# The order of the middle groups' steps on four engines, in a four-layer kernel on one Trainium2 core

## The chip, the core and the metric

The kernel runs as one program on one core of a Trainium2 chip. The metric is the device time of one execution in microseconds (us). The engines are named as the profile names them: PE (TensorE; PEld its weight loads), DVE (VectorE), ACT (ScalarE), POOL (GpSimd), SP (the queue that loads and stores). Each works through its own instructions in order and waits for the others at semaphores.

## What is computed

Four layers over an input of 16 sequences of 256 tokens with 128 features. Each layer's output is normed and added to its input. Cut to what matters:

```python
x = x + norm(conv(norm(x)))          # a long convolution along the tokens, one decaying complex mode per feature
x = x + norm(moe(norm(x)))           # 8 routed experts (the best 2 by softmax) and a shared one, silu(x Wg) * (x Wu) Wd
x = x + norm(attention(norm(x)))     # 16 heads of 64, q and k of unit length, ALiBi, causal, 2 null keys
x = x + norm(four_experts(norm(x)))  # router (best 2 of 4) over a gated MLP, two chains of matrices, a gelu MLP
```

In the fourth layer all four experts are computed for every token and weighed by `pick1`, which is zero for those not chosen.

## The kernel before

The 16 sequences are worked in 8 groups of 2 (512 tokens, four tiles of 128). A group passes through the four layers, whose steps bear the letters `e` (convolution), `l` (routed experts), `a` (attention) and `f` (four experts). The layers of different groups are interleaved: while the list plays group g's attention, it plays the fourth layer of group g-1 and the expert layer and convolution of groups g+1 and g+2. For each engine a list of step names, written out by hand in tables at the top of the file, sets the order of its instructions. `play` (L702) goes through a list and calls each step; `plan` (L707) plays `PROLOGUE` and `FIRST` once, `MIDDLE` five times (groups 1 to 5), then `LAST_L`, `LAST_A` and `LAST_F`:

```python
for i in range(1, G - 2):
    play(steps, table(MIDDLE[name]), e=i + 2, l=i + 1, a=i, f=i - 1)
```

A step does the same in whatever place it stands, and waits for its inputs at semaphores; the lists set only what is queued ahead of what. The steps that matter here:

- `a_m`, `a_k`, `a_v` (PE, three products of 512 columns for each half): projections to queries, keys and values, into three PSUM banks in turn; `a_t` turns the unit queries. ACT empties each bank.
- `l_turn3`: PE turns the normed tile of the expert layer (L1784), ACT copies it (L1112), DVE takes the rest below fp32r (L1477). The routing and all of the expert layer follow from it. It needs `l_norm` (DVE, L1399 `xn<-x`).
- `l_route`, `l_pick`, `l_coef`: router products on PE (L1778, L1779), the best two on DVE (L1495 to L1505), their weights (L1511 to L1525).
- `f_out.t` (t = 0 to 3): PE computes the outputs of the four experts for tile t (L2229 to L2235), DVE adds them up weighted (L1723, four instructions). The first of these starts from the biases that POOL's `f_bias` has weighed and added (L983, L987). `f_bias` needs the routing weights (`f_pick`, DVE, L1693 to L1705) and `l_norm`.
- `f_end_stats`, `f_end`: norm of the fourth layer's sum and the residual (L1399 `x4m`, L1404).
- `a_nexp` (DVE, L1592 and L1594, then ACT, L1183): the null keys' exponentials; `a_nT` turns them.
- `a_scores.c` (c = 0 to 7, a unit of four heads of one sequence): PE's scores in four 64x64 tiles (L2036, L2042), ACT's exponentials (L1199 to L1208), POOL's causal masks and the addition of the late keys (L952, L962). `a_mix.c`: PE's sums and mixes (L2091 to L2105), then DVE's division (L1609 to L1623). PE's scores of the next unit need ACT's exponentials of this one; PE's mix of the next unit needs DVE's division of this one.
- `l_g`, `l_u`, `l_c` (PE) with `l_hg`, `l_hu`, `l_hc` (DVE): gate, up and coefficient of the expert layer, five times; `l_c` is one product over 72 rows (L1930). `l_down`, `a_out`: the output products.
- `e_stats`, `e_apply`, `e_scan`, `e_sum`: norm and scan of the convolution two groups ahead; POOL's `e_scan` is two products (L923). `a_keep` is POOL's copy of a layer's input (L933). `a_kss`, `a_ss` are POOL's roots for keys and queries (L943, L937).

At the end of the list the attention input is normed (`l_aapply`), turned (`l_x`, L1951), split (`l_xl`, DVE, L1477 `xaT_lo`), and the next `a_m.0` starts.

Of the kernel before, what the change touches and what calls it, by code (L numbers as in the profile page):

```python
# [83 lines left out]

MIDDLE = {
    "PE": """
a_m.0 a_m.1 a_k.0 f_turn.0 f_turn.1 a_null f_ce.0 f_ce.1 a_k.1 f_sw.0 f_me.0 a_kr.0 a_t.0 f_ceT a_m.2 f_sw.1 a_k.2
f_relu.0 a_k.3 f_sw.2 a_t.1 a_m.3 f_relu.1 a_kr.1 f_sw.3 a_kt f_ce2 f_me.1 l_turn2 a_v.0 a_t.2 f_ml.0 a_v.1 f_ml.1
a_t.3 f_ce2T f_ml.2 f_ml.3 a_v.2 a_v.3 l_turn3 f_out.0 l_route f_out.1 a_scores.0 a_nT f_out.2 l_g.0 f_out.3
a_scores.1 l_u.0 l_g.1 l_cT a_mix.0 a_scores.2 a_mix.1 e_turn1 l_u.1 a_scores.3 l_g.2 l_c.0 l_u.2 a_mix.2 a_scores.4  # L90
a_mix.3 l_g.3 l_u.3 a_scores.5 l_c.1 l_g.4 a_mix.4 a_scores.6 l_u.4 l_c.2 a_mix.5 l_c.3 a_scores.7 a_mix.6 l_down.0
l_down.1 l_down.2 a_mix.7 l_down.3 a_out.0 a_out.1 l_x.0 l_x.1
""",
    "DVE": """
f_stats.0 f_stats.1 f_apply.0 f_apply.1 a_ss.0 f_turn.0 a_null f_turn.1 f_ce f_route a_u.0 f_ce_apply f_hid.0 a_ss.1
a_ss.2 f_hid.1 a_u.1 f_pick a_u.2 f_hid.2 a_ss.3 a_kss f_hid.3 f_ce2 l_turn2 a_u.3 f_ce2_apply l_res l_norm l_turn3
e_stats a_nexp l_route l_pick l_coef f_out.0 a_nT f_out.1 l_hg.0 f_out.2 f_out.3 f_end_stats e_apply a_mix.0 l_hu.0
l_hg.1 a_mix.1 l_cT l_hu.1 e_scan a_mix.2 l_hg.2 l_hu.2 a_mix.3 l_hc.0 l_hg.3 l_hc.1 e_sum l_hu.3 a_mix.4 l_hc.2
a_mix.5 l_hg.4 l_hu.4 l_hc.3 a_mix.6 f_end l_dstats.0 a_mix.7 l_end.0 l_dstats.1 l_astats.0 l_end.1 a_o.0 l_astats.1
a_end.0 l_aapply.0 l_aapply.1 a_o.1 l_xl.0 l_xl.1 a_end.1  # L100
""",
    "ACT": """
a_m.0 a_m.1 f_turn.0 f_turn.1 a_k.0 a_k.1 f_me.0 f_sw.0 a_t.0 f_pick f_ceT a_m.2 f_sw.1 a_k.2 f_relu.0 a_k.3 a_t.1
f_sw.2 a_m.3 a_ks f_relu.1 f_sw.3 a_v.0 a_t.2 f_ml.0 a_v.1 f_ml.1 a_t.3 f_ce2T f_ml.2 f_ml.3 a_v.2 f_me.1 l_turn3
a_nexp a_v.3 l_exp a_scores.0 l_g.0 a_scores.1 l_g.1 l_cT a_scores.2 a_scores.3 l_g.2 a_scores.4 l_g.3 a_scores.5
a_scores.6 l_g.4 a_scores.7 l_x.0 l_x.1
""",
    "POOL": """
f_stats.0 f_stats.1 a_ss.0 f_ce a_ss.1 a_ss.2 f_ce_apply a_ss.3 f_ce2 l_turn2 a_kss.0.0 l_res a_kss.0.1 f_bias
a_kss.1.0 e_stats a_kss.1.1 a_scores.0 a_keep a_scores.1 a_scores.2 a_scores.3 e_scan a_scores.4 f_end_stats  # L110
a_scores.5 a_scores.6 a_scores.7 l_dstats.0 l_dstats.1 l_astats.0 a_o.0 l_astats.1 a_o.1
""",
}

# [2162 lines left out]
```

## Time and profile before

| what | us |
|---|---|
| median of 3 runs (lowest to highest) | 929.02 (928.15 to 929.4) |
| the profiled execution | 928.41 |
| its span, first to last instruction | 926.6 |
| what lies around the span | 1.8 |
| busy: PE / DVE / POOL / ACT | 860.1 / 779.7 / 587.7 / 586.2 |
| mean granted TensorE clock | 0.991 of full speed |

The span holds a prologue, the first group, the five middle groups of some 106.5 us each, and the three closing lists. Busy time is what an engine's instructions cover; matmuls are pipelined, so a busy PE need not be at its peak. DMA plays a part at the start only: over the span HBM is used at 11 GB/s.

### The profile page before, as it was taken

What the parts mean: (1) busy time and instruction counts of PE and PEld (TensorE: products, weight loads), DVE (VectorE), ACT (ScalarE), POOL (GpSimd) and SP (SyncE); (2) the same over time, 40 slices, a digit from 0 to 9 for tenths busy, and PEclk for the clock granted to TensorE, in tenths of its full rate; (3) what the DMA queues carried; (4) which work ended last, traced back from release to release, by engine and by line L of the source; (5) the groups of instructions that cost most, each with busy time, mean ns of one, the idle gap of its engine ahead of it and who ended that gap; (6) DMA issues with size and microseconds to landing.
All of it is one profiled execution on the core that took longest, in us unless ns stands there. A gap on an engine that the chain in (4) does not pass through costs nothing.

```text
span 926.6 us, 25509 instructions
## 1 busy us (share of the span) xinstructions
PE 860.1 (93%) x10110; PEld 700.6 (76%) x10110; DVE 779.7 (84%) x2457; ACT 586.2 (63%) x1255; POOL 587.7 (63%) x632
## 2 busy tenths in 40 slices
...
DMA packets 22008, 11.73 MB, mean 13 GB/s; under 512 B 7552, under 2 KB 21248, under 8 KB 21760
## 3 DMA queue, kind: packets, MB, share of 16 engines
...
## 4 chain that ended last, share of the span: by engine, by line
PE 49%; DVE 38%; ACT 7%; issue 4%; POOL 2%; DMA 0%; DVEq 0%; ACTq 0%; POOLq 0%
PE bank L1771 8%; PE bank L1772 7%; PE bank L1773 7%; PE bank L1784 5%; DVE x4m L1723 3%; PE bank L2036 3%; DVE qT L1623 2%; DVE mixed L1620 2%; PE bank L2042 2%; PE bank L1999 2%; PE bank L2204 1%; DVE bank L1609 1%; DVE xn L1399 1%; PE bank L2211 1%; DVE conv L1451 1%
## 5 line engine op out<-in xcount | busy, mean ns | idle before, releaser
L937 POOL TENSOR_TENSOR rnorm<-sumsq,minus_half 128x16 f32<-128x16 f32 x32 | 95.4, 2990 | 55.6 <-DVE sumsq L1574 55.3
L943 POOL TENSOR_TENSOR rnorm<-unit,minus_half 128x16 f32<-128x16 f32 x32 | 93.1, 2916 | 3.1 <-DVE unit L1580 3.1
L1202 ACT ACTIVATE square<-bank,bias_k,rnorm 128x256 f32<-128x256 f32 x128 | 65.7, 570 | 44.8 <-PE bank L2036 44.8
L2042 PE MATMUL bank<-qT,kT 64*64 64x64 f32 (+1 forms) x1024 | 82.9, 253 | 5.6 <-ACT unit L1208 3.3
L2036 PE MATMUL bank<-qT,kT 64*64 64x256 f32 (+1 forms) x1024 | 84.4, 358 | 0.0
L952 POOL TENSOR_SCALAR_AFFINE_SELECT square<-square 128x256 f32<-128x256 f32 x128 | 61.8, 509 | 34.3 <-ACT square L1208 34.3
L1132 ACT ACTIVATE xaT_hi<-bank 128x256 fp32r<-128x256 f32 x16 | 6.0, 384 | 115.3 <-PE bank L1951 114.7
L952 POOL TENSOR_SCALAR_AFFINE_SELECT unit<-unit 128x256 f32<-128x256 f32 x128 | 48.5, 407 | 37.9 <-ACT unit L1208 37.9
L2042 PEld LDWEIGHTS bank<-qT,kT 64*64 64x64 f32 x1024 | 51.9, 132 | 20.8 <-ACT unit L1208 6.9
L2118 PE MATMUL bank<-w_out,qT 128*128 128x128 f32 x512 | 62.8, 276 | 1.5 <-DVE qT L1623 1.5
L1202 ACT ACTIVATE unit<-bank,bias_k,rnorm 128x256 f32<-128x256 f32 x96 | 51.5, 575 | 17.7 <-PE bank L2036 16.3
L2118 PEld LDWEIGHTS bank<-w_out,qT 128*128 128x128 f32 x512 | 59.7, 192 | 2.3 <-DVE qT L1623 1.7
L2036 PEld LDWEIGHTS bank<-qT,kT 64*64 64x64 f32 x1024 | 55.1, 132 | 5.3
L1208 ACT ACTIVATE unit<-bank,bias_k,rnorm 128x128 f32<-128x128 f32 x128 | 52.8, 479 | 0.0
L1208 ACT ACTIVATE square<-bank,bias_k,rnorm 128x128 f32<-128x128 f32 x128 | 52.4, 473 | 0.0
L1175 ACT ACTIVATE val<-bank 128x512 f32<-128x512 f32 x64 | 37.1, 595 | 24.2 <-PE bank L1773 22.0
L1784 PEld LDWEIGHTS bank<-ident,unit 128*128 128x128 f32 x296 | 34.6, 143 | 18.0 <-DVE unit L1588 11.7
L901 POOL TENSOR_TENSOR n_d_rstd<-n_d_var,minus_half 128x2 f32<-128x2 f32 x16 | 11.7, 732 | 57.3 <-DVE n_d_var L1415 57.2
L1571 DVE TENSOR_REDUCE sumsq<-square 128x16 f32<-128x1024 f32 x32 | 38.9, 1215 | 10.1 <-ACT square L1148 10.1
L1141 ACT ACTIVATE unit<-bank 128x512 f32<-128x512 f32 x64 | 36.9, 605 | 16.5 <-PE bank L1773 15.3
L1784 PE MATMUL bank<-ident,unit 128*128 128x128 f32 x296 | 40.6, 279 | 6.2 <-DVE unit L1588 5.3
L1623 DVE TENSOR_TENSOR qT<-bank,mixed 128x512 f32<-128x512 f32 x64 | 44.2, 691 | 2.2
...
## 6 DMA issues: line engine op xcount, KB each, us to landing
...
```

Of the source, the lines that this page charges most:

```text
L937: pool.tensor_tensor(rnorm[:, 1, t, :], sumsq[:, t % 2, :], minus_half[:], ALU.pow).then_inc(a_root.sem, 1)
L943: pool.tensor_tensor(rnorm[:, 0, ts, hs], k_sumsq[:, ts, hs], minus_half[:, hs].unsqueeze(1).to_broadcast([P, 2, H // 2]), ALU.pow).then_i ...
L952: pool.affine_select(out=pd, in_=pd, compare_op=ALU.is_ge, fill=0.0, base=0, pattern=[[0, 2], [step, P]], channel_multiplier=-step).then_i ...
L1202: last = act.activation(early(pr, j), k0, ACT.Exp, bias=bias_k0[:, h:h + 1], scale=by)
L1208: last = act.activation(late(pr, j), bank[2][:, 2 * P * s + P * j:2 * P * s + P * (j + 1)], ACT.Exp, bias=bias_k1[:, h:h + 1], scale=by)
L1771: mm(dst, left.hi, right.hi, start=True, stop=False)
L1772: mm(dst, left.hi, right.lo, start=False, stop=False)
L1773: return mm(dst, left.lo, right.hi, start=False, stop=True)
L1784: last = nc.tensor.transpose(dst[:, t * P:(t + 1) * P], src(t), ident[:])
L2036: return mm(bank[s][cs, 2 * P * (i + 1) - n:2 * P * (i + 1)], kT[rs, p, 2 * P * b + 64 * k:2 * P * b + 64 * k + 64], qT[rs, p, 2 * P * (b ...
L2042: return mm(bank[2][cs, 2 * P * s + P * i:2 * P * s + P * i + n], kT[rs, p, tile1 + 64 * k:tile1 + 64 * k + 64], qT[rs, p, tile1:tile1 + n ...
L2118: mm(out_bank(g, h)[:, ts], outT[:, c, ts], w_out[:, c, :], start=(c == 0), stop=False)
```

## The change

The table `MIDDLE` is replaced by another order of the same steps, for PE, DVE, ACT and POOL. Nothing else changes: the other lists, the steps, the scores in four tiles and the coefficients over 72 rows stay. The order in which the banks for `a_m`, `a_k`, `a_t` and `a_v` are taken in turn (it is read from PE's list) comes out the same, and so does the mix ahead of which PE turns the next convolution's input (`e_turn1`, after two mixes). The lines of the diff that the text speaks of:

```diff
 MIDDLE = {
     "PE": """
-a_m.0 a_m.1 a_k.0 f_turn.0 f_turn.1 a_null f_ce.0 f_ce.1 a_k.1 f_sw.0 f_me.0 a_kr.0 a_t.0 f_ceT a_m.2 f_sw.1 a_k.2
+a_m.0 a_m.1 a_null a_k.0 f_turn.0 f_turn.1 f_ce.0 f_ce.1 a_k.1 f_sw.0 f_me.0 a_kr.0 a_t.0 a_m.2 f_ceT f_sw.1 a_k.2
...
-a_t.3 f_ce2T f_ml.2 f_ml.3 a_v.2 a_v.3 l_turn3 f_out.0 l_route f_out.1 a_scores.0 a_nT f_out.2 l_g.0 f_out.3
+f_ce2T a_t.3 a_v.2 f_ml.2 f_ml.3 a_v.3 f_out.0 l_turn3 f_out.1 l_route a_scores.0 l_g.0 f_out.2 f_out.3 a_nT
...
     "DVE": """
...
-e_stats a_nexp l_route l_pick l_coef f_out.0 a_nT f_out.1 l_hg.0 f_out.2 f_out.3 f_end_stats e_apply a_mix.0 l_hu.0
+l_turn3 e_stats f_out.0 l_route l_pick f_out.1 l_hg.0 l_coef f_out.2 f_out.3 f_end_stats a_nT a_mix.0 l_hg.1 e_apply
...
     "POOL": """
-f_stats.0 f_stats.1 a_ss.0 f_ce a_ss.1 a_ss.2 f_ce_apply a_ss.3 f_ce2 l_turn2 a_kss.0.0 l_res a_kss.0.1 f_bias
-a_kss.1.0 e_stats a_kss.1.1 a_scores.0 a_keep a_scores.1 a_scores.2 a_scores.3 e_scan a_scores.4 f_end_stats
+f_stats.0 f_stats.1 a_ss.0 f_ce a_ss.1 a_ss.2 f_ce_apply a_ss.3 a_kss.0.0 f_ce2 l_turn2 a_kss.0.1 l_res f_bias
+a_kss.1.0 e_stats a_kss.1.1 a_scores.0 a_scores.1 a_scores.2 a_scores.3 e_scan a_keep a_scores.4 a_scores.5
```


On PE, ahead of the score units, where the third middle group leaves the value projections and turns the expert layer's input (`xn`). Before:

```order
L1771 MATMUL bank<-w_kv_hi,xaT_hi 128x512
L1772 MATMUL bank<-w_kv_lo,xaT_hi 128x512
L1773 MATMUL bank<-w_kv_hi,xaT_lo 128x512
L1784 MATMUL bank<-ident,xn 128x128 x4
L2229 MATMUL bank<-w_sw,mixed 128x128 x4
L2231 MATMUL bank<-w_c,mixed 128x128 x2
L2233 MATMUL bank<-w_gen,x4m 128x128
L2235 MATMUL bank<-w_ml,square 128x128 x4
```


And now:

```order
L1771 MATMUL bank<-w_kv_hi,xaT_hi 128x512
L1772 MATMUL bank<-w_kv_lo,xaT_hi 128x512
L1773 MATMUL bank<-w_kv_hi,xaT_lo 128x512
L2229 MATMUL bank<-w_sw,mixed 128x128 x4
L2231 MATMUL bank<-w_c,mixed 128x128 x2
L2233 MATMUL bank<-w_gen,x4m 128x128
L2235 MATMUL bank<-w_ml,square 128x128 x4
L1784 MATMUL bank<-ident,xn 128x128 x4
```


The four products of `f_out.0` (L2229 to L2235) have gone ahead of the turning of `xn`.

On DVE, from `l_norm` (L1399 `xn<-x`) of the same group to the first weighted sums (L1723). Before:

```order
L1399 TENSOR_SCALAR xn<-x,n_l_mv,n_l_rstd 128x128 x4
L1477 TENSOR_TENSOR xlT_lo<-bank,xlT_hi 128x512
L1389 BN_STATS n_x_six<-xin 128x6 x4
L1392 BN_AGGR n_x_mv<-n_x_six 128x2 x4
L1394 TENSOR_SCALAR n_x_var<-n_x_mv 128x4
L1592 TENSOR_TENSOR null_s<-null_s,rnorm 128x128
L1594 SCALAR_TENSOR_TENSOR null_s<-null_s,bias_null 128x128
L1495 TENSOR_REDUCE logit<-bank 128x32
L1501 MAX top<-logit 128x8 x4
L1504 MAX_INDEX idx<-top,logit 128x8 x4
L1505 TENSOR_TENSOR exp<-top 128x32
L1511 CAST idf<-idx 128x8
```


And now:

```order
L1399 TENSOR_SCALAR xn<-x,n_l_mv,n_l_rstd 128x128 x4
L1592 TENSOR_TENSOR null_s<-null_s,rnorm 128x128
L1594 SCALAR_TENSOR_TENSOR null_s<-null_s,bias_null 128x128
L1477 TENSOR_TENSOR xlT_lo<-bank,xlT_hi 128x512
L1389 BN_STATS n_x_six<-xin 128x6 x4
L1392 BN_AGGR n_x_mv<-n_x_six 128x2 x4
L1394 TENSOR_SCALAR n_x_var<-n_x_mv 128x4
L1723 SCALAR_TENSOR_TENSOR x4m<-bank,pick,ce_rows 128x128
L1723 SCALAR_TENSOR_TENSOR x4m<-bank,pick,x4m 128x128 x3
L1495 TENSOR_REDUCE logit<-bank 128x32
L1501 MAX top<-logit 128x8 x4
L1504 MAX_INDEX idx<-top,logit 128x8 x4
```


`a_nexp` (L1592, L1594) has gone ahead of `l_turn3` (L1477), and `f_out.0` (L1723) ahead of the router's reduction and pick (L1495 to L1505).

On POOL, from the query roots to the biases (L983, L987) of the same group. Before:

```order
L937 TENSOR_TENSOR rnorm<-sumsq,minus_half 128x16
L894 TENSOR_TENSOR n_c_rstd<-n_c_var,minus_half 128x4
L894 TENSOR_TENSOR n_y_rstd<-n_y_var,minus_half 128x4
L943 TENSOR_TENSOR rnorm<-unit,minus_half 128x2x8
L894 TENSOR_TENSOR n_l_rstd<-n_l_var,minus_half 128x4
L943 TENSOR_TENSOR rnorm<-unit,minus_half 128x2x8
```


And now:

```order
L937 TENSOR_TENSOR rnorm<-sumsq,minus_half 128x16
L943 TENSOR_TENSOR rnorm<-unit,minus_half 128x2x8
L894 TENSOR_TENSOR n_c_rstd<-n_c_var,minus_half 128x4
L894 TENSOR_TENSOR n_y_rstd<-n_y_var,minus_half 128x4
L943 TENSOR_TENSOR rnorm<-unit,minus_half 128x2x8
L894 TENSOR_TENSOR n_l_rstd<-n_l_var,minus_half 128x4
```


The first key root (L943) has gone ahead of the roots for `f_ce2` (`n_c_rstd`) and `l_turn2` (`n_y_rstd`), and the second ahead of that for `l_res` (`n_l_rstd`).

## Rows read from the trace of the kernel before

**Rows 1.** The page's head: busy time of each engine (share of the span).
```profile
PE 860.1 (93%) x10110; PEld 700.6 (76%) x10110; DVE 779.7 (84%) x2457; ACT 586.2 (63%) x1255; POOL 587.7 (63%) x632
```

**Rows 2.** Three middle groups: start:end, length, busy us of PE, PEld, DVE, ACT, POOL, clock.
```profile
140.70:247.10 106.40, 103.45 (x1296) 84.22 (x1295) 95.23 (x300) 72.30 (x156) 74.22 (x76) 1.00 0.02 5
247.11:353.25 106.14, 103.09 (x1246) 84.17 (x1245) 95.42 (x303) 70.24 (x150) 71.79 (x73) 1.00 0.02 7
...
459.65:566.76 107.11, 104.35 (x1249) 85.69 (x1248) 95.87 (x303) 70.26 (x150) 71.91 (x73) 0.98 0.02 7
```

**Rows 3.** The same view, the two parts of the third middle group.
```profile
369.47:410.65 41.18, 41.03 (x217) 30.79 (x218) 35.88 (x121) 35.38 (x67) 26.04 (x15) 1.00 0.03 8
410.65:475.80 65.15, 62.36 (x1032) 53.67 (x1031) 59.72 (x181) 34.85 (x83) 45.97 (x59) 1.00 0.02 6
```

**Rows 4.** PE's longest wait in four middle groups: us in total, times, longest.
```profile
PE bank L1771 <- DVE xaT_lo L1477: 3.1, 4, 0.8
```

**Rows 5.** Order of time, third middle group, DVE: start, us, instruction [idle before it].
```profile
409.42 1.12 DVE L1399 TENSOR_SCALAR xn<-x,n_l_mv,n_l_rstd 128x128 f32<-128x128 f32 x4 [1.12 <-POOL n_l_rstd L894]
411.91 0.69 DVE L1477 TENSOR_TENSOR xlT_lo<-bank,xlT_hi 128x512 fp32r<-128x512 f32 x1 [1.38 <-ACT xlT_hi L1112]
...
414.21 0.28 DVE L1592 TENSOR_TENSOR null_s<-null_s,rnorm 128x128 f32<-128x128 f32 x1
...
415.69 0.21 DVE L1495 TENSOR_REDUCE logit<-bank 128x32 f32<-128x64 f32 x1
...
416.90 1.23 DVE L1505 TENSOR_TENSOR exp<-top 128x32 f32<-128x32 f32 x1
...
419.12 0.29 DVE L1522 TENSOR_TENSOR pick<-pick,prob 128x32 f32<-128x32 f32 x2
...
452.89 0.69 DVE L1539 TENSOR_TENSOR unit<-unit,bank 128x512 f32<-128x512 f32 x1 [0.44 <-PE bank L1930]
...
459.57 2.50 DVE L1399 TENSOR_SCALAR x4m<-x4m,n_f_mv,n_f_rstd 128x128 f32<-128x128 f32 x4
```

**Rows 6.** The same view, PE: start of `f_out.0`, and of the router's products.
```profile
411.08 1.06 PE L2229 MATMUL bank<-w_sw,mixed 128*128 128x128 f32 x8
...
413.46 0.26 PE L1778 MATMUL bank<-w_router,xlT_hi 128*128 128x16 f32 x1
```

**Rows 7.** The same view, POOL: roots, biases (first and last of five), the copy.
```profile
396.77 2.91 POOL L937 TENSOR_TENSOR rnorm<-sumsq,minus_half 128x16 f32<-128x16 f32 x1 [2.28 <-DVE sumsq L1574]
401.27 1.01 POOL L894 TENSOR_TENSOR n_c_rstd<-n_c_var,minus_half 128x4 f32<-128x4 f32 x1 [1.59 <-DVE n_c_var L1394]
...
412.21 1.05 POOL L983 TENSOR_TENSOR ce_rows<-row_out,pick 128x512 f32<-128x512 f32 x1
...
416.82 1.27 POOL L987 TENSOR_TENSOR ce_rows<-ce_rows,x 128x512 f32<-128x512 f32 x1
418.05 2.91 POOL L943 TENSOR_TENSOR rnorm<-unit,minus_half 128x16 f32<-128x16 f32 x1
...
427.56 0.61 POOL L933 COPY x<-x2n 128x512 f32<-128x512 f32 x1
```

**Rows 8.** The same view, DVE, in the group behind the middle ones (list LAST_L).
```profile
731.58 1.11 DVE L1399 TENSOR_SCALAR xn<-x,n_l_mv,n_l_rstd 128x128 f32<-128x128 f32 x4 [0.60 <-POOL n_l_rstd L894]
...
738.89 0.35 DVE L1723 SCALAR_TENSOR_TENSOR x4m<-bank,pick,ce_rows 128x128 f32<-128x128 f32 x1 [2.68 <-POOL ce_rows L987]
...
772.38 0.47 DVE L1609 STREAM_TRANSPOSE bank<-bank 128x256 f32<-128x256 f32 x1 [1.80 <-PE bank L2094]
...
776.39 1.44 DVE L1399 TENSOR_SCALAR x4m<-x4m,n_f_mv,n_f_rstd 128x128 f32<-128x128 f32 x4
```

**Rows 9.** The same view, DVE, first middle group: the pick's last step, its successor.
```profile
204.07 0.17 DVE L1505 TENSOR_TENSOR exp<-top 128x32 f32<-128x32 f32 x1
204.28 1.12 DVE L1511 CAST idf<-idx 128x8 f32<-128x8 uint32 x1
```

**Rows 10.** As rows 2: where the fourth group begins its projections.
```profile
475.80:480.00 4.20, 4.20 (x12) 3.29 (x13) 3.59 (x16) 2.54 (x5) 1.70 (x3) 0.60 0.00 0
```

More of the change, by code:

```diff
@@ L92 @@
-l_down.1 l_down.2 a_mix.7 l_down.3 a_out.0 a_out.1 l_x.0 l_x.1
+a_m.0 a_m.1 a_null a_k.0 f_turn.0 f_turn.1 f_ce.0 f_ce.1 a_k.1 f_sw.0 f_me.0 a_kr.0 a_t.0 a_m.2 f_ceT f_sw.1 a_k.2
+a_k.3 f_relu.0 f_sw.2 a_t.1 a_m.3 a_kr.1 f_relu.1 f_sw.3 a_kt f_ce2 a_v.0 l_turn2 f_ml.0 f_ml.1 a_t.2 a_v.1 f_me.1
+f_ce2T a_t.3 a_v.2 f_ml.2 f_ml.3 a_v.3 f_out.0 l_turn3 f_out.1 l_route a_scores.0 l_g.0 f_out.2 f_out.3 a_nT
+a_scores.1 l_u.0 l_g.1 a_mix.0 a_scores.2 a_mix.1 l_u.1 e_turn1 l_g.2 a_scores.3 a_mix.2 l_u.2 l_cT a_scores.4
```

27 lines of the change are left out of this document (12 added, 15 removed).

## The prediction

> **What bounds the kernel now.** I read the page first, then the stretches group by group, then the waits, then the order in time of one group. By the page PE is busy 860 of 926.6 us and DVE 780 [rows 1], so neither is free as an average. The five middle groups, whose lists change, each take 106.1 to 107.1 us, with PE busy about 103.4 and DVE about 95.5 [rows 2]. They repeat, so I work in one of them, from its first query projection (369.47) to that of the next (475.80).
>
> It has two parts [rows 3]. From 369.47 to 410.65 PE is busy 41.03 of 41.18 us and DVE 35.88: PE alone sets the pace, until it turns the normed tile in `l_turn3`. From there to 475.80 DVE is busy 59.72 of 65.15 us as the profile counts, and its order of time has two marked gaps, 0.31 and the 0.44 of [rows 5]; the chain of waits follows DVE there. PE is nearly as full (62.36). Its longest wait there is 0.8, at the handover to the next group, once in each of four [rows 4]. So a step moved out of the second part helps if it is DVE's, and a step moved into the first part hurts if it is PE's. This change does one of each.
>
> **The change part by part.** No instruction is added or removed; 5 groups are reordered. All terms are us per group.
>
> 1. *PE computes `f_out.0` ahead of `l_turn3`.* Before, `l_turn3` starts at 410.65 [rows 3], `f_out.0` runs from 411.08 and the router's products start at 413.46 [rows 6]. These 2.4 us now lie at the end of the part that PE sets, and all that DVE does after `l_turn3` starts as much later: **+2.4**.
>
> 2. *The other swaps ahead of `l_turn3`* (`a_null`, `f_ceT`, `f_relu`, `f_me.1`, `f_ml`, `a_v` change places). PE's sum is the same; PE has 0.15 us to gain there (41.18 less 41.03). It can lose: POOL now takes the root `a_kss.0.0` ahead of `f_ce2`'s. Such a root takes 2.91, and POOL had 1.59 idle ahead of `f_ce2`'s at 401.27 [rows 7], so that this one comes 1.3 later. DVE has `a_u.3` to do in between, and PE's `f_ce2T`, which needs what follows, has a dozen products queued ahead of it. Bounds -0.15 to +1.3, taken **0**.
>
> 3. *DVE does `a_nexp` ahead of `l_turn3`.* From 414.21 to 415.69 it took 1.48 [rows 5]; now it runs while PE is still busy with term 1, where DVE waits anyway. **-1.5**.
>
> 4. *`f_out.0` goes ahead of the router's pick on DVE.* The last step of `l_pick` took 1.23 us [rows 5] and 0.17 in the first middle group [rows 9]; it began at 416.90, beside POOL's addition of the biases that began at 416.82 and took 1.27 [rows 7]. Since `f_out.0` needs the sum of these biases, `l_pick` now comes after that addition, beside the root that POOL takes next (2.91). Beside such a root DVE is not held: `l_coef`'s two products of 419.12, with two SBUF inputs each, took 0.29 together [rows 5] within the root of 418.05 to 420.96 [rows 7]. **-1.1**, bounds -1.1 to 0. The Trainium skill (SBUF — State Buffer, "Who interferes with whom") says that a DVE instruction with two SBUF inputs and a POOL instruction that reads SBUF exclude each other for the whole instruction. That agrees with the 1.23 beside the addition; for the root it says the opposite of the row above, and speaks against this change. By it the term would be about +0.9, as `l_coef` would have to wait (last rival).
>
> 5. *`f_out.0` waits for POOL's biases.* They take 412.21 to 418.05, 5.84 us [rows 7], and need `l_norm`, which ended at 410.54 (409.42 + 1.12) [rows 5]. In the group behind the middle ones, whose list has the same order here, `f_out.0` began at 738.89, 6.2 us after `l_norm`'s end (731.58 + 1.11), having waited 2.68 [rows 8]. Now `l_norm` ends between 410.54 and 411.5, an estimate: `f_pick` is put ahead of it, where DVE waited 1.12, and some of term 2's 1.3 arrives. So the sum is ready at 416.7 to 417.7. DVE gets there at 411.91 + 2.4 + 2.3 (`l_turn3` and `e_stats`, 411.91 to 414.21) = 416.6. Bounds +0.1 to +1.1, taken **+0.5**.
>
> 6. *`f_end` ahead of `a_mix.6`.* It took 2.50 us [rows 5], and 1.44 where the last-but-one list has it at the same place [rows 8]. POOL's masks of the last unit now fall beside it, so I take half: **-0.5**, bounds -1.1 to 0.
>
> 7. *The chain scores, exponentials, masks, mix.* POOL's copy `a_keep` (0.61) [rows 7] moves from ahead of unit 1 to between the products of `e_scan` and unit 4's masks, and PE's `a_mix.4` is queued behind it, and DVE's behind that. PE's `a_mix.0` also finds `a_nT` directly ahead of it on DVE, where six steps had stood between. Bounds: -0.75, if nothing new waits and the 0.31 and 0.44 go, to +1.8, the longest wait of this chain in the next list [rows 8]. Taken **+0.6**, the copy.
>
> ACT's and SP's moves are covered: ACT is busy 70 of 106 us [rows 2], and no DMA is nearer its use than before. The end of the group (`l_dstats.1` ahead of `l_end.0`, `l_aapply.0` ahead of `a_end.0`) has the same DVE steps before the next projections: 0.
>
> Sum: 2.4 + 0 - 1.5 - 1.1 + 0.5 - 0.5 + 0.6 = **+0.4 a group, +2.0 for five**. The profiled execution took 928.41, 0.61 under the median of the runs shown (929.02), and so would take 930.4; against the median that is **931.0 us**.
>
> **Rivals.**
>
> *Faster: DVE's relief all arrives.* `f_out.0` finds the biases ready (+0.1), `f_end` runs in 1.44 (-1.1), and the chain gains nothing and loses nothing: 2.4 - 1.5 - 1.1 + 0.1 - 1.1 = -1.2 a group, **923.0**. PE's own work allows it: it idles 2.9 us a group (0.15 and 65.15 less 62.36) [rows 3], of which 0.8 at the handover stays [rows 4], so the floor is -2.1. It decides at `f_out.0`: where `l_norm` ends by 410.6, nothing else stands ahead of DVE until unit 4. For it: `l_pick` lies beside a root almost surely. Against it: every wait I left out adds.
>
> *Slower: the relief is given back.* In the first middle group the pick's last step took 0.17, not 1.23, but the next instruction took 1.12 in its place [rows 9], and the group took 106.40, no less than the next one's 106.14 [rows 2]. If terms 4 and 6 are lost like that: 2.4 - 1.5 + 0.5 + 0.6 = +2.0 a group, **939.0**. For it: two nearly full engines and POOL's long additions beside them. Against it: after the bias sum POOL has nothing but three roots to do, two of them of 2.91 [rows 7].
>
> *A slower clock.* In the fourth group TensorE ran at 0.60 of full speed from 475.80 for 4.2 us, part of it at its lower level of 1.2 GHz, after the handover's short waits [rows 10], and that group took 107.11, 0.7 more [rows 2]. More idle PE at this place could make it so in each group: 3.5 more, **934.5**. The other groups with the same waits stayed at 1.00.
>
> *POOL's roots hold DVE.* Then `l_coef`, which follows 4 to 6 us behind the bias sum, waits for the end of `a_kss.1.1`, about 2 us a group: **941**. The Trainium skill's rule of term 4 would have it so; but in this kernel `l_coef`'s products already lie beside such a root, and took 0.29 (term 4).
>
> **How the numbers follow.** The forecast has 0.48, and its own range is 928.5 to 934.0 (terms 2, 5 and 7 by half their bounds). The faster rival has 0.25, the relief given back 0.20, the clock 0.04, the roots 0.03. A measurement tells 0.2% from no change, 1.86 us, so faster ends at 927.2 and slower begins at 930.9. Of the forecast 0.28 is slower and 0.20 within; of the faster rival 0.22 is faster and 0.03 within; the others are slower: 0.22, 0.23, 0.55. The range of 923.5 to 939.5 leaves out about 0.1 on either side.
>
> **What would show it.** `l_turn3` starts 43.5 to 44.0 us after the first projections, not 41.2 (terms 1, 2). DVE waits for POOL's biases by 0.1 to 1.1 ahead of `f_out.0`, behind an `e_stats` (terms 3, 5). The pick's last step takes 0.17 to 0.2 (4), `f_end` 1.4 to 2.5 (6). From `l_turn3` to the next group 62 to 64 us pass, not 65.15. If that is 61.6 or less, the faster rival holds; at 65 or more the relief was given back, and the row where it went is the one to look for. If `l_turn3` is not later by 2, the first term is wrong and with it the sign.

## The result, and the profile after

The changed kernel takes **923.74 us** (median of 4 runs, 922.4 to 924.23) against 928.81 for the kernel before: ratio 0.9943, 95% interval 0.9926 to 0.9961. That is 5.1 us faster, where 931.0 and slower was forecast; the range of 923.5 to 939.5 just holds it. The rival that I called faster gave 923.0.

The page's head and the stretches of the changed kernel, to be held against [rows 1 to 3] (three of the five middle groups, then the two parts of the third; columns as there):

```profile
PE 861.8 (93%) x10110; PEld 697.6 (76%) x10110; DVE 765.4 (83%) x2457; ACT 586.3 (64%) x1255; POOL 581.3 (63%) x632
```

```profile
156.90:262.47 105.57, 103.86 (x1247) 84.06 (x1247) 92.81 (x302) 70.23 (x150) 70.70 (x73) 1.00 0.02 7
...
368.03:473.55 105.52, 103.87 (x1246) 84.05 (x1246) 92.77 (x302) 70.24 (x150) 70.70 (x73) 1.00 0.03 7
...
579.09:684.66 105.57, 103.88 (x1247) 84.07 (x1247) 92.75 (x302) 70.23 (x150) 70.68 (x73) 1.00 0.02 7
...
368.03:412.09 44.06, 43.75 (x238) 33.09 (x239) 37.52 (x123) 35.33 (x67) 29.48 (x18) 1.00 0.03 7
412.09:473.55 61.46, 60.12 (x1010) 50.96 (x1008) 55.24 (x179) 34.91 (x83) 41.22 (x56) 1.00 0.03 7
```

All five groups now take 105.5 to 105.6. Cut at the first query projections, as in [rows 3], the third took 106.33 before, so a group is 0.8 shorter: the first part grew by 2.88 (41.18 to 44.06), the second shrank by 3.69 (65.15 to 61.46). DVE is busy 2.8 less per group, 4.5 less in the second part. Five times 0.8 is 4.0; the fourth group's stretch at a lower clock in the profiled execution of before [rows 10], about 0.8, makes up the 4.8 by which the five groups together differ (532.56 and 527.76). Whether that stretch comes in every execution of before no profile shows, so 0.8 of the 4.8 can't be put down to the order with certainty.

PE's waits in the second to fifth middle group of both kernels, first of before (us in total, times, longest; the second view also takes in the handover behind the last group), show who sets the second part now:

```profile
PE bank L2091 <- DVE qT L1623: 4.3, 8, 0.6
PE bank L1771 <- DVE xaT_lo L1477: 3.1, 4, 0.8
PE bank L1951 <- DVE ce_rows L1421: 2.1, 4, 0.6
```

```profile
PE bank L1771 <- DVE xaT_lo L1477: 3.9, 5, 0.8
PE bank L2091 <- DVE conv L1446: 1.3, 4, 0.3
PE bank L2139 <- ACT conv L1214: 1.0, 4, 0.3
```

In before PE waited twice a group for a mix that DVE had not finished (`qT`), and once near the end (`ce_rows`); after, only the handover and two waits of 0.3 are left, of which that for ACT's `conv` lies in the first part (`f_ce.0`, which no longer has `a_null` ahead of it). PE is busy 60.12 of 61.46 us there: the second part has become PE's. PE now idles 1.7 us a group in place of 2.9, while the group is 0.8 shorter: for the same products PE counts as busy 0.5 longer (103.39 and 103.87), and no run shows why.

The order of time, DVE, third middle group of the changed kernel, has the steps that were priced: `l_norm`, `a_nexp`'s long step, `l_turn3`, `f_out.0`, `l_pick`'s last step, `l_coef`'s products, the mix of unit 4, `f_end`.

```profile
408.23 1.12 DVE L1399 TENSOR_SCALAR xn<-x,n_l_mv,n_l_rstd 128x128 f32<-128x128 f32 x4
...
409.58 1.13 DVE L1594 SCALAR_TENSOR_TENSOR null_s<-null_s,bias_null 128x128 f32<-128x128 f32 x1
413.36 0.69 DVE L1477 TENSOR_TENSOR xlT_lo<-bank,xlT_hi 128x512 fp32r<-128x512 f32 x1 [2.65 <-ACT xlT_hi L1112]
...
415.57 0.35 DVE L1723 SCALAR_TENSOR_TENSOR x4m<-bank,pick,ce_rows 128x128 f32<-128x128 f32 x1
...
418.22 0.17 DVE L1505 TENSOR_TENSOR exp<-top 128x32 f32<-128x32 f32 x1
...
421.08 0.30 DVE L1522 TENSOR_TENSOR pick<-pick,prob 128x32 f32<-128x32 f32 x2
...
447.25 0.47 DVE L1609 STREAM_TRANSPOSE bank<-bank 128x256 f32<-128x256 f32 x1 [0.78 <-PE bank L2094]
...
455.94 1.25 DVE L1399 TENSOR_SCALAR x4m<-x4m,n_f_mv,n_f_rstd 128x128 f32<-128x128 f32 x4
```

And POOL beside them: the root that was put ahead of `f_ce2`'s, the biases (first and last), the two roots behind them, then the last addition ahead of `f_end` and the masks beside it.

```profile
398.14 2.91 POOL L943 TENSOR_TENSOR rnorm<-unit,minus_half 128x16 f32<-128x16 f32 x1
...
409.52 1.05 POOL L983 TENSOR_TENSOR ce_rows<-row_out,pick 128x512 f32<-128x512 f32 x1 [1.32 <-DVE xn L1399]
...
414.18 1.28 POOL L987 TENSOR_TENSOR ce_rows<-ce_rows,x 128x512 f32<-128x512 f32 x1
415.41 2.91 POOL L943 TENSOR_TENSOR rnorm<-unit,minus_half 128x16 f32<-128x16 f32 x1
...
419.27 2.90 POOL L943 TENSOR_TENSOR rnorm<-unit,minus_half 128x16 f32<-128x16 f32 x1
...
454.29 1.28 POOL L962 TENSOR_TENSOR mixed<-unit 128x512 f32<-128x512 f32 x1
456.70 0.77 POOL L952 TENSOR_SCALAR_AFFINE_SELECT square<-square 128x256 f32<-128x256 f32 x2 [1.14 <-ACT square L1208]
```

The biases start as soon as `l_norm` ends and are summed at 415.46; DVE reaches `f_out.0` at 415.5 and does not wait. Before, the root `a_kss.0.1` of 2.9 stood between `l_res` and the biases (they begin at its end, the 412.21 of [rows 7]); now both roots of `a_kss.0` come ahead of `l_res`. The root in before:

```profile
409.35 2.90 POOL L943 TENSOR_TENSOR rnorm<-unit,minus_half 128x16 f32<-128x16 f32 x1
```

### The profile page after: what moved, and what is told of

Same layout as the page of the kernel before. It is cut to its first block, busy times and chain, and to the rows that moved or that the text cites. A ratio compares the mean times of both kernels' runs of the same rounds, so it can differ in the third digit from the quotient of the medians.

```text
span 922.0 us, 25509 instructions
## 1 busy us (share of the span) xinstructions
PE 861.8 (93%) x10110; PEld 697.6 (76%) x10110; DVE 765.4 (83%) x2457; ACT 586.3 (64%) x1255; POOL 581.3 (63%) x632
## 4 chain that ended last, share of the span: by engine, by line
PE 59%; DVE 21%; ACT 12%; POOL 4%; issue 3%; DMA 0%; DVEq 0%; POOLq 0%; ACTq 0%
PE bank L1771 8%; PE bank L1772 7%; PE bank L1773 7%; PE bank L1784 4%; PE bank L2036 4%; PE bank L1937 3%; PE bank L2229 3%; PE bank L2235 3%; PE bank L2042 2%; PE bank L2204 2%; DVE xn L1399 1%; PE bank L2211 1%; PE bank L2105 1%; PE bank L2103 1%; PE bank L2101 1%
## 5 line engine op out<-in xcount | busy, mean ns | idle before, releaser
L943 POOL TENSOR_TENSOR rnorm<-unit,minus_half 128x16 f32<-128x16 f32 x32 | 93.2, 2919 | 3.1 <-DVE unit L1580 3.1
L952 POOL TENSOR_SCALAR_AFFINE_SELECT square<-square 128x256 f32<-128x256 f32 x128 | 55.1, 454 | 54.0 <-ACT square L1208 53.9
L1588 DVE TENSOR_TENSOR unit<-unit,rnorm 128x1024 f32<-128x1024 f32 x32 | 44.5, 1389 | 13.0 <-POOL rnorm L937 13.0
L1168 ACT ACTIVATE qT<-bank,qk_scale 128x512 f32<-128x512 f32 x64 | 40.8, 693 | 16.4 <-PE bank L1784 16.3
L1784 PEld LDWEIGHTS bank<-ident,unit 128*128 128x128 f32 x296 | 34.4, 143 | 16.9 <-DVE unit L1588 11.3
L1784 PE MATMUL bank<-ident,unit 128*128 128x128 f32 x296 | 40.6, 279 | 6.1 <-DVE unit L1588 5.3
```

The costliest lines, as they stand in the source:

```text
L943: pool.tensor_tensor(rnorm[:, 0, ts, hs], k_sumsq[:, ts, hs], minus_half[:, hs].unsqueeze(1).to_broadcast([P, 2, H // 2]), ALU.pow).then_i ...
L952: pool.affine_select(out=pd, in_=pd, compare_op=ALU.is_ge, fill=0.0, base=0, pattern=[[0, 2], [step, P]], channel_multiplier=-step).then_i ...
L1784: last = nc.tensor.transpose(dst[:, t * P:(t + 1) * P], src(t), ident[:])
```

## The experiments

All edit the table of the middle groups only; the diffs show the stretch of a list that an edit touches, and not the whole list. The table gives the median, the ratio to the kernel before, run beside each (its medians are 927.96 to 928.81), with its 95% interval, and one middle group (the third, for pool_back the second and for four_edits the first) with its two parts, cut as in [rows 3].

| kernel | us | ratio | group = first + second part |
|---|---|---|---|
| before | 928.81 | | 106.33 = 41.18 + 65.15 |
| changed | 923.74 | 0.9943 (0.9926 to 0.9961) | 105.52 = 44.06 + 61.46 |
| fend_only | 924.11 | 0.9949 (0.9932 to 0.9965) | 105.70 = 41.19 + 64.51 |
| fend_back | 925.81 | 0.9967 (0.9953 to 0.9981) | 106.19 = 44.10 + 62.09 |
| four_edits | 937.05 | 1.0086 (1.0070 to 1.0103) | 107.53 = 43.73 + 63.80 |
| pool_back | 930.95 | 1.0021 (1.0010 to 1.0033) | 106.71 = 44.09 + 62.62 (the second) |
| fout_back | 922.58 | 0.9927 (0.9910 to 0.9944) | 105.36 = 41.60 + 63.76 |
| nexp_only | 928.35 | 0.9994 (0.9984 to 1.0004) | 106.13 = 41.18 + 64.95 |
| hybrid_null | 930.53 | 1.0022 (1.0007 to 1.0037) | 106.61 = 41.28 + 65.33 |
| ao_late | 928.93 | 0.9993 (0.9980 to 1.0005) | 106.32 = 45.09 + 61.23 |
| tail_only | 921.75 | 0.9924 (0.9906 to 0.9942) | 105.21 = 41.18 + 64.03 |
| head_only | 930.71 | 1.0024 (1.0014 to 1.0034) | 106.48 = 44.07 + 62.41 |
| keep_back | 923.60 | 0.9944 (0.9926 to 0.9962) | 105.55 = 44.08 + 61.47 |
| hybrid2 | 920.43 | 0.9911 (0.9893 to 0.9929) | 105.06 = 41.27 + 63.79 |
| eapply | 925.97 | 0.9965 (0.9952 to 0.9979) | 106.04 = 41.19 + 64.85 |
| lct | 927.31 | 0.9983 (0.9973 to 0.9992) | 106.34 = 41.21 + 65.13 |
| both | 929.05 | 1.0001 (0.9991 to 1.0011) | 106.52 = 41.20 + 65.32 |
| pairs | 924.70 | 0.9964 (0.9950 to 0.9978) | 105.74 = 41.16 + 64.58 |
| pairs_back | 923.57 | 0.9954 (0.9937 to 0.9971) | 105.68 = 41.20 + 64.48 |

Two things keep the medians from being compared to a microsecond. The first group, whose list nobody edits, took 91.0 to 93.2 us in the profiled executions, at a granted clock of 0.93 to 0.96. And some middle groups ran at a lower clock: three in four_edits, two in pool_back, one each in head_only, hybrid_null, nexp_only and before. The text therefore compares groups.

### f_end, taken alone and given back

fend_only, in the kernel before, and fend_back, in the changed one, move the same step on DVE:

```diff
-l_hc.3 a_mix.6 f_end l_dstats.0
+l_hc.3 f_end a_mix.6 l_dstats.0
```

```diff
-l_hu.4 f_end a_mix.6 l_dstats.0
+l_hu.4 a_mix.6 f_end l_dstats.0
```

> Kernel before, with f_end put ahead of a_mix.6 on DVE and nothing else. Theory (DVE's relief: POOL's 1.26 us addition in L962 holds the last of f_end's four products, and one unit earlier there is no such addition beside it): f_end takes 1.25 to 1.45 us in place of 2.50, and each of five groups gets 1.0 to 1.25 shorter, 922.5 to 924. My prediction's choice (half of it, masks beside it): 926.3. Rival (PE is the bound and the time came from the order of PE's own list): f_end may be short, the time stays within 1 us of 928.8.

> Changed kernel, with f_end put back behind a_mix.6 on DVE. Theory (DVE's relief): f_end takes 2.3 to 2.5 us again beside POOL's addition for the last unit; DVE had 0.62 us of waiting right behind it, which covers a part, so each group gets 0.5 to 1.25 longer: 926.2 to 930. Rival (PE is the bound): the wait covers it, 923 to 924.5.

A group got 0.63 shorter with the one (106.33 to 105.70) and 0.67 longer with the other (105.52 to 106.19); by time, fend_only is nearly as fast as the whole change, and fend_back, at 925.81, lies just under its expected 926.2. Both are less than the 1.0 to 1.25 of full relief, and more than nothing. `f_end` itself went from 2.50 to 1.35 us, and back from 1.25 to 2.39. It is long where POOL's addition lies beside it; in the order of time of fend_back, DVE and POOL:

```profile
460.16 2.39 DVE L1399 TENSOR_SCALAR x4m<-x4m,n_f_mv,n_f_rstd 128x128 f32<-128x128 f32 x4
...
461.21 1.27 POOL L962 TENSOR_TENSOR mixed<-square 128x512 f32<-128x512 f32 x1
```

`f_end` ends at 462.55, the addition at 462.48. Ahead of `a_mix.6` only masks lie beside it. Half of the 1.15 arrives: behind it DVE then waits 0.40 (fend_only) or 0.62 (changed) for PE's products of the last mix. On PE the gain is the wait near the end of the group, for `ce_rows`: 2.1 us in four groups of before, none in fend_only or the changed kernel, and back in fend_back:

```profile
PE bank L1951 <- DVE ce_rows L1421: 2.3, 4, 0.6
```

### Four moves without their companions, and POOL's list put back

four_edits takes the kernel before and makes the moves that terms 1 and 3 to 6 priced:

```diff
-a_v.3 l_turn3 f_out.0 l_route f_out.1
+a_v.3 f_out.0 l_turn3 l_route f_out.1
-l_res l_norm l_turn3 e_stats a_nexp l_route l_pick l_coef f_out.0 a_nT
+l_res l_norm a_nexp l_turn3 e_stats f_out.0 l_route l_pick l_coef a_nT
-l_hc.3 a_mix.6 f_end l_dstats.0
+l_hc.3 f_end a_mix.6 l_dstats.0
```

> Kernel before, with only the four moves that my sum priced: on PE f_out.0 ahead of l_turn3, on DVE a_nexp ahead of l_turn3, f_out.0 ahead of l_route, f_end ahead of a_mix.6. POOL's list is the one of before, so its bias sum is ready 48.6 us after the group's first projection (47.4 in the changed kernel, where a_kss.0.0 goes ahead of f_ce2's root). Theory (the POOL move is what let f_out.0 go without a wait): DVE waits 1.0 to 1.5 us for POOL ahead of f_out.0, and a group takes 105.5 plus up to 1.5: 924 to 930. Rival (the other moves are worth nothing): 923 to 924.5, with no wait on POOL.

pool_back is the changed kernel with POOL's list of before:

```diff
-a_ss.3 a_kss.0.0 f_ce2 l_turn2 a_kss.0.1
+a_ss.3 f_ce2 l_turn2 a_kss.0.0
-l_res f_bias
+l_res a_kss.0.1 f_bias
-a_scores.0 a_scores.1 a_scores.2 a_scores.3 e_scan a_keep a_scores.4 a_scores.5 f_end_stats
+a_scores.0 a_keep a_scores.1 a_scores.2 a_scores.3 e_scan a_scores.4 f_end_stats a_scores.5
```

> Changed kernel, with POOL's list of the kernel before (a_kss.0.0 behind l_turn2, a_keep ahead of unit 1, f_end_stats ahead of unit 5). Theory (POOL's move is what let f_out.0 go without a wait): DVE waits about 1.2 us for the bias sum in each group; PE had about 0.6 us of idle time besides the handover, so 0.5 to 1.2 a group longer: 926 to 930. Rival (POOL's moves are covered, as I took them): 923 to 924.5.

Both lost more than expected. In pool_back, third middle group, a root of 2.90 stands between `l_norm` and the biases again (POOL), and DVE waits 1.44 for their sum in every group (DVE):

```profile
409.37 2.90 POOL L943 TENSOR_TENSOR rnorm<-unit,minus_half 128x16 f32<-128x16 f32 x1
...
416.85 1.27 POOL L987 TENSOR_TENSOR ce_rows<-ce_rows,x 128x512 f32<-128x512 f32 x1
```

```profile
418.24 0.35 DVE L1723 SCALAR_TENSOR_TENSOR x4m<-bank,pick,ce_rows 128x128 f32<-128x128 f32 x1 [1.44 <-POOL ce_rows L987]
```

Behind it PE waits 1.05 to 1.09, and a group takes 106.7, 1.2 more than in the changed kernel; two of its five groups took 108.3, with TensorE's clock below full speed for some us behind that place (last section). In four_edits DVE waits the same 1.43, and PE waits besides, because without `f_out.1` between them the router's products stand directly behind `l_turn3` (PE):

```profile
417.10 0.28 PE L1778 MATMUL bank<-w_router,xlT_hi 128*128 128x16 f32 x1 [1.41 <-DVE xlT_lo L1477]
```

So the moves that I priced are, without the others, a loss of 1.2 a group (the first, 107.53 for 106.34; at the lower clock 108.3 to 108.4), where terms 1 and 3 to 6 summed to -0.2. What POOL's list is worth pool_back shows; PE's `f_out.1` was not moved alone.

### The swap on PE, and a_nexp alone

fout_back, in the changed kernel (PE), and nexp_only, in the kernel before (DVE):

```diff
-a_v.3 f_out.0 l_turn3 f_out.1
+a_v.3 l_turn3 f_out.0 f_out.1
```

```diff
-l_res l_norm l_turn3 e_stats a_nexp l_route
+l_res l_norm a_nexp l_turn3 e_stats l_route
```

> Changed kernel, with PE doing l_turn3 ahead of f_out.0 again; DVE still takes f_out.0 ahead of l_route. If term 1 is a cost that could simply be had back, l_turn3 starts 41.6 us after the group's first projection in place of 44.06 and the group gets shorter by up to what PE idles there (1.7 us, of which 0.8 is the handover): 919 to 921. My theory (POOL's bias sum, ready at 47.4 to 47.6 after the first projection, is what DVE meets at f_out.0, and so f_out.0 on PE costs nothing where it now stands): l_turn3 starts at 41.6, DVE waits 2.3 to 2.7 us on POOL ahead of f_out.0, the group keeps its 105.5: 923 to 924.5.

> Kernel before, with a_nexp ahead of l_turn3 on DVE and nothing else. DVE gets 1.48 us out of the part it fills, and l_pick's last step starts 1.5 us earlier, mostly between POOL's long additions, which gives up to 1.06 more; but f_out.0 then meets the bias sum, ready 48.6 us after the first projection, where DVE stood at 50.1. Theory (relief counts up to the next wait): f_out.0 starts at 48.6, a group gets 0.7 to 1.5 shorter: 921.5 to 925.5. Rival (PE's order sets the time, not DVE): 927.5 to 929.5.

fout_back did as the theory said: `l_turn3` at 41.60, and DVE waiting in the place of PE:

```profile
415.94 0.35 DVE L1723 SCALAR_TENSOR_TENSOR x4m<-bank,pick,ce_rows 128x128 f32<-128x128 f32 x1 [2.56 <-POOL ce_rows L987]
```

The group got 0.16 shorter, and the median, 922.58, lies 0.4 under the theory's band: nearly no change. nexp_only gave 0.20 instead of 0.7 to 1.5. Its time lies in the rival's band, but the trace shows another reason than PE's order: DVE's relief was given back. The second step of `a_nexp` had taken 1.24 beside a POOL addition (414.35 to 415.62); moved, it took 0.29 (first before, then nexp_only):

```profile
414.52 1.24 DVE L1594 SCALAR_TENSOR_TENSOR null_s<-null_s,bias_null 128x128 f32<-128x128 f32 x1
410.86 0.29 DVE L1594 SCALAR_TENSOR_TENSOR null_s<-null_s,bias_null 128x128 f32<-128x128 f32 x1
```

`l_pick`'s last step fell to 0.17 too, but two steps behind it (0.17 and 0.26 in before) became long in its place, each to the end of a POOL instruction (DVE, then POOL; 416.96 beside 416.94, 418.4 beside 418.28):

```profile
415.85 0.17 DVE L1505 TENSOR_TENSOR exp<-top 128x32 f32<-128x32 f32 x1
416.06 0.90 DVE L1511 CAST idf<-idx 128x8 f32<-128x8 uint32 x1
...
417.18 1.25 DVE L1517 TENSOR_TENSOR pick<-expert_no,idf 128x32 f32<-128x32 f32 x2
```

```profile
415.79 1.15 POOL L983 TENSOR_TENSOR x<-row_out,pick 128x512 f32<-128x512 f32 x1
417.01 1.27 POOL L987 TENSOR_TENSOR ce_rows<-ce_rows,x 128x512 f32<-128x512 f32 x1
```

DVE came to `f_out.0` only 0.63 earlier in its group, and to the first mix 0.26. In these runs the pick and its weights were free of such holds where they came behind the whole sum, as in the changed list; ahead of it the pick's last step took 0.75 even in the best kernel below (hybrid2).

### First halves and second halves crossed

tail_only has before's lists up to the first scores (DVE: up to `f_end_stats`) and the changed ones from there; head_only the reverse. `a_nT` stays where its half has it. For PE, tail_only reads, up to unit 4 (`-` is before):

```diff
-a_scores.1 l_u.0 l_g.1 l_cT a_mix.0 a_scores.2 a_mix.1 e_turn1 l_u.1 a_scores.3 l_g.2 l_c.0 l_u.2 a_mix.2 a_scores.4
-a_mix.3 l_g.3 l_u.3 a_scores.5 l_c.1 l_g.4 a_mix.4
+a_scores.1 l_u.0 l_g.1 a_mix.0 a_scores.2 a_mix.1 l_u.1 e_turn1 l_g.2 a_scores.3 a_mix.2 l_u.2 l_cT a_scores.4
+a_mix.3 l_g.3 l_u.3 l_c.0 a_scores.5 l_g.4 a_mix.4 l_c.1
```

> Kernel before with the second half of the changed kernel's four lists: PE and ACT from a_scores.1 on, DVE behind f_end_stats, POOL from a_scores.0 on; the first halves are those of before. Theory (the first halves cancel, the gain is f_end's 0.6 a group and some 0.5 more out of the chain of scores, masks and mixes, my term 7 with its other sign): groups of 105.0 to 105.4, 921 to 923.5. My prediction's terms 6 and 7: minus 0.5 plus 0.6, 929. Rival (DVE's relief in the first half carries it, here only f_end is left): 924 to 925, as with f_end alone.

> The other cross: the changed kernel's first halves (f_out.0, a_nexp, l_pick, POOL's root, a_null) with the second halves of before. Theory: my terms 1 to 5 as measured, 2.88 less 1.48 less 1.06, so 0.3 a group slower than before, 106.4 to 107.0, 928.5 to 932. Rival (DVE's relief in the first half carries the gain): 924.5 to 927.

As the theory said: the second halves alone give 1.12 a group, 0.31 more than the whole change; the first halves alone cost 0.15 a group (one of the five took 108.05, at a lower clock, and so the time is 2.5 over the 928.20 of before run beside it). Together they would be -0.97, and the change is -0.81, so the halves do not quite add up. In tail_only PE's waits for `qT` and `ce_rows` are gone (all its waits, four groups):

```profile
PE bank L1771 <- DVE xaT_lo L1477: 3.1, 4, 0.8
PE bank L2091 <- DVE conv L1446: 1.3, 4, 0.3
PE bank L2042 <- ACT val L1175: 0.7, 4, 0.2
```

keep_back then tests the price in term 7 that was hung on POOL's copy:

```diff
-a_scores.0 a_scores.1 a_scores.2 a_scores.3 e_scan a_keep a_scores.4
+a_scores.0 a_keep a_scores.1 a_scores.2 a_scores.3 e_scan a_scores.4
```

> Changed kernel with POOL's copy a_keep back ahead of unit 1, nothing else. It tests the 0.6 us that I charged in term 7. Theory (PE is the bound by then; the copy delays unit 4's masks and DVE's next mix, and PE has scores and products to do meanwhile): DVE's wait of 0.78 us at the mix of unit 4 shrinks to 0.1 to 0.3, the groups keep 105.4 to 105.6: 923 to 924.5. By my term 7 a group would get 0.6 shorter: 920.7.

The time stayed, as expected, but not for the reason given: DVE's wait did not shrink either.

```profile
447.90 0.47 DVE L1609 STREAM_TRANSPOSE bank<-bank 128x256 f32<-128x256 f32 x1 [0.78 <-PE bank L2094]
```

With or without the copy ahead of unit 4's masks it is 0.78: PE comes to these products when its own queue lets it, with no wait on POOL.

### What in the second halves gives the other 0.5

f_end gives 0.63 of the 1.12. fend_only's PE still has the two waits for DVE's mixes (0.54 at unit 1, 0.57 at unit 3). eapply, lct and both add to it the moves that should end them (eapply the first pair of lines, lct the others, DVE and then PE; on ACT lct has `l_cT` behind `a_scores.3`):

```diff
-f_end_stats e_apply a_mix.0
+f_end_stats a_mix.0 e_apply
-a_mix.1 l_cT l_hu.1 e_scan a_mix.2 l_hg.2 l_hu.2 a_mix.3 l_hc.0 l_hg.3 l_hc.1
+a_mix.1 l_hu.1 e_scan a_mix.2 l_cT l_hg.2 l_hu.2 a_mix.3 l_hg.3 l_hc.0 l_hc.1
-l_g.1 l_cT a_mix.0 a_scores.2 a_mix.1 e_turn1 l_u.1 a_scores.3 l_g.2 l_c.0 l_u.2 a_mix.2 a_scores.4 a_mix.3 l_g.3 l_u.3
+l_g.1 a_mix.0 a_scores.2 a_mix.1 e_turn1 l_u.1 a_scores.3 l_g.2 l_u.2 a_mix.2 l_cT a_scores.4 a_mix.3 l_g.3 l_u.3 l_c.0
```

> Kernel before with f_end ahead of a_mix.6 and e_apply behind a_mix.0 on DVE, two moves. With f_end alone a group took 105.7 and PE waited 0.54 us at the mix of unit 1 and 0.57 at that of unit 3, both for DVE's mix before. Theory (the second halves' gain is DVE's mixes coming earlier for PE): the first of the two waits goes, a group takes 105.2 to 105.5. Rival (PE meets the same time further on): 105.6 to 105.8 with another wait in its place.

> Kernel before with f_end ahead of a_mix.6, and l_cT put behind a_mix.2 (PE and DVE; behind a_scores.3 on ACT), with l_c.0 and l_hc.0 moved behind it. Theory: DVE's mix of unit 2 comes 0.7 us earlier, PE's wait of 0.57 at unit 3's mix goes, a group takes 105.1 to 105.5 instead of 105.7. Rival (the coefficients then come late for l_c.0 and DVE waits there): 105.6 or more.

> Kernel before with all three: f_end, e_apply and l_cT moved. Theory: these three are what the second halves give; a group takes 105.1 to 105.3, as with the whole second halves (105.2), and the time is 921 to 922.5. If it stays over 105.4, another of the moves in the second halves carries part of it.

All three got slower than fend_only: the theory fell. The waits aimed at were gone, but PE's waits in both show longer ones further on, at `e_turn1` (L1784) and at `l_c.1` (L1930):

```profile
PE bank L1784 <- DVE den L1614: 3.9, 4, 1.0
PE bank L1771 <- DVE xaT_lo L1477: 3.1, 4, 0.8
PE bank L1930 <- DVE unit L1539: 3.0, 4, 0.7
```

In the changed list PE has `l_u.1` ahead of `e_turn1`, and `l_g.4` and `a_mix.4` ahead of `l_c.1`. pairs adds this to both; pairs_back takes it out of tail_only:

```diff
-a_mix.1 e_turn1 l_u.1
+a_mix.1 l_u.1 e_turn1
-l_c.1 l_g.4 a_mix.4
+l_g.4 a_mix.4 l_c.1
-l_hc.1 e_sum l_hu.3 a_mix.4 l_hc.2
+l_hu.3 a_mix.4 l_hc.1 e_sum l_hc.2
```

```diff
-a_mix.1 l_u.1 e_turn1
+a_mix.1 e_turn1 l_u.1
-a_scores.5 l_g.4 a_mix.4 l_c.1
+a_scores.5 l_c.1 l_g.4 a_mix.4
```

> The kernel with f_end, e_apply and l_cT moved, plus the steps that its trace shows PE stuck at: on PE e_turn1 goes behind l_u.1 and l_c.1 behind a_mix.4, on DVE l_hc.1 and e_sum behind a_mix.4. Theory (a DVE step moved behind a mix pays only if PE's step that meets the mix's result or its bank gets other work ahead of it): PE's waits of 0.98 at e_turn1 and 0.74 at l_c.1 go, a group takes 105.1 to 105.5, 920.5 to 923. Rival (the gain needs more of the second half, such as l_hu.4 and the last steps): 106 or more.

> The kernel with all of the changed second halves, with two PE steps put back to where before has them: e_turn1 directly behind a_mix.1, l_c.1 ahead of l_g.4 and a_mix.4. DVE's list is left as it is. Theory: PE waits 0.6 to 1.0 at e_turn1 for DVE's mix, and 0.3 to 0.8 at l_c.1; a group takes 105.8 to 106.5 in place of 105.2, 924.5 to 928. Rival (DVE's order alone carries the gain): 921 to 922.5.

pairs won back 0.78 of a group (106.52 to 105.74), which is no more than fend_only; pairs_back lost 0.47, in the expected direction and a little less than its band: PE waits 0.39 at `e_turn1` and 0.22 and 0.21 at two `l_c`. So these PE steps carry about 0.5 where DVE's list is the changed one, and the moves of both are a loss without them. The whole second halves are 0.5 better than pairs; which of the remaining moves (the order of `l_hg`, `l_hu` and `e_sum` among the mixes, `l_u.4`, the last statistics) gives that was not tried further.

### Tries at a better version

hybrid_null and hybrid2 turn `l_turn3` first again and fill the wait for the biases that fout_back showed with the router. Edits of the changed kernel; the PE line marked 2 is hybrid2's, the rest is common:

```diff
-a_m.1 a_null a_k.0 f_turn.0 f_turn.1 f_ce.0
+a_m.1 a_k.0 f_turn.0 f_turn.1 a_null f_ce.0
-f_out.0 l_turn3 f_out.1 l_route
+l_turn3 f_out.0 f_out.1 l_route
+l_turn3 f_out.0 l_route f_out.1   (2)
-f_apply.0 a_null f_apply.1 a_ss.0 f_turn.0 f_turn.1
+f_apply.0 f_apply.1 a_ss.0 f_turn.0 a_null f_turn.1
-e_stats f_out.0 l_route l_pick f_out.1
+e_stats l_route l_pick f_out.0 f_out.1
```

> Changed kernel with three moves: PE does l_turn3 ahead of f_out.0, DVE does l_route and l_pick ahead of f_out.0 (so that they fill the wait for POOL's biases), and a_null goes back behind f_turn on PE and DVE (PE waits 0.26 us on ACT's conv in the changed kernel, 0 before). Theory: f_out.0 starts at 47.4 to 47.8 with the pick already done, DVE gains 1.2 to 1.5 us a group, and PE, busy 103.9 of 105.5 with 0.8 at the handover, lets 0.3 to 0.9 of it through: 919.5 to 922.5. Rival (the pick's last step is held beside the bias additions, 1.23 for 0.17, and what follows it is late): 923 to 925.

> A try at a version that beats both: changed kernel, PE does l_turn3, f_out.0, l_route, f_out.1; DVE does l_route and l_pick ahead of f_out.0, in the time in which it waits for POOL's biases; a_null is back behind f_turn on PE and DVE. The earlier try lost 3.0 us of DVE's time a group to l_route, which stood behind f_out.1 on PE; here it doesn't. Theory: l_turn3 at 41.3 us, l_route at 45.2 to 45.5 with a wait under 0.7, f_out.0 at 47.4 to 47.8 with the pick done, and groups of 104.5 to 105.1: 918.5 to 921.5. Rival (PE waits for the banks of f_out.1 or the later steps as it did in that try): 923 or more.

hybrid_null lost, outside both of its bands: the router's products were behind `f_out.1` on PE, and DVE waited 2.96 for them (`L1495`). hybrid2, with that one step turned, took **920.43 us**, the lowest median of all (0.9911, with an interval that still overlaps tail_only's): its groups of 105.06 lie inside the 104.5 to 105.1 expected. ao_late moves a step on DVE ahead of the handover:

```diff
-l_aapply.1 a_o.1 l_xl.0 l_xl.1 a_end.1
+l_aapply.1 l_xl.0 l_xl.1 a_o.1 a_end.1
```

> Changed kernel, with a_o.1 behind l_xl.0 and l_xl.1 on DVE. PE's handover wait of 0.77 us in each group ends with DVE's xaT_lo, which has a_o.1's 0.9 us directly ahead of it and starts 0.2 us after ACT's half is there. Theory (PE is now the bound, and only this wait and one of 0.33 are left): the wait falls to 0.5 to 0.6, the group by 0.15 to 0.25: 922.3 to 923.2. If DVE still set the time, a_o.1 would only move and the time stay at 923.5 to 924.

The handover's wait fell from 0.8 to 0.5 and the second part from 61.46 to 61.23, as expected, but the next group's first part grew by 1.03 (44.06 to 45.09): what DVE put off is what PE's `f_turn` then waits for, and the time, 928.93, missed both of its bands (PE's waits, four groups):

```profile
PE bank L1945 <- DVE x4m L1421: 3.6, 8, 0.5
PE bank L1771 <- DVE xaT_lo L1477: 2.0, 4, 0.5
```

## Why the prediction was wrong

**The step that failed is term 7**, the chain of scores, masks and mixes. It was taken at +0.6, "the copy"; the crossed halves give -0.49 for it in the kernel before (-1.12 less `f_end`'s -0.63), and -0.29 in the changed one (105.52 less head_only's 106.48, less `f_end`'s -0.67). Those 0.9 to 1.1 us a group, 4.5 to 5.5 in all, are most of the 6.6 between the 930.4 that the sum gave for the profiled execution and its 923.83, and they turned the sign. The copy costs nothing (keep_back): I had carried POOL's delay on to DVE's mix and from there to the group's end, while in that stretch PE sets the time. The gain that I allowed only as a bound (-0.75) was marked by PE's waits for DVE's mixes, 4.3 us in four groups, which stand in the same view as [rows 4] and are not among my rows; I had read the chain on DVE alone. DVE's own gaps there did not mark it: the 0.31 (ahead of the L1539 at 447.68) and the 0.44 went, others of 0.78 and 0.62 came, and the group got shorter. Which moves make this gain is known in part: the two PE steps of pairs_back carry 0.47 of it in tail_only's list, but added to both they gave no more than fend_only.

*Term 1, +2.4:* the first part grew by 2.88. `l_turn3` came later by `f_out.0`'s own length (409.60 to 412.09 on PE, 2.49), plus 0.4, most of which belongs to *term 2*: with `a_null` back behind `f_turn` the first part is 0.32 shorter (41.60 in fout_back, 41.28 in hybrid_null). But as a cost that could be had back, it is 0.16 (fout_back): with `l_turn3` first DVE would wait for the biases.

*Term 2, POOL's root, 0:* I saw it only as something that could be late. It lets the other root go ahead of `l_res`, out of the way of the biases, and without POOL's list a group is 1.2 longer (pool_back; the copy in it costs nothing).

*Term 3, -1.5:* `a_nexp` left the second part, but most of the 1.48 was not its own length: its second step was long beside POOL's addition, and alone the move gave 0.20 (nexp_only). That this step took 1.13 in its new place did no harm: DVE waits 2.65 behind it.

*Term 4, -1.1:* right, 1.23 became 0.17. `l_coef`'s two products took 0.30 at 421.08, inside the root of 419.27 to 422.17. By the rule of the Trainium skill (SBUF — State Buffer, "Who interferes with whom") they would have been held to its end; here the measurement decides, for the roots. For POOL's additions the trace agrees with the rule: two products beside one of them took 1.25 in nexp_only (L1517), and 0.26 in before beside a root.

*Term 5, +0.5:* 0. The sum was ready at 415.46 and DVE there at 415.5. `l_norm` ended 41.3 us after the first projection, in the range I gave; the late `l_turn3` covered the rest.

*Term 6, -0.5:* 0.63 to 0.67, near, by another way: `f_end` got 1.15 to 1.25 back, since the masks beside it hardly held it (1.25 to 1.35), and DVE's next wait for PE swallowed half.

Terms 1 to 5 together were +0.3 a group; head_only measured +0.15, and the changed kernel less tail_only +0.31. The forecast's own range does not follow from its bounds: with terms 2, 5 and 7 half way to them it would be about 926 to 939. Of the rivals, the faster one named the right place (`f_out.0` without a wait), and by its sign (61.6 or less from `l_turn3` on) it holds with 61.46. That its time was only 0.7 off is luck: it had `f_end` at -1.1 for -0.6 to -0.7 and the chain at nothing for -0.3 to -0.5, and these cancel. The relief given back did not happen in this list, but it is what nexp_only shows. The slower clock did not come in the changed kernel's middle groups, and the roots did not hold `l_coef`.
